# Two copies moved inside ScalarE's odd slots of a graph and attention kernel

## The reference, cut to what matters

```
x = x + gnn(layernorm(x), edges) + mix(layernorm(x))     # 100000 edges, two graph layers
x = x + ffn(layernorm(x))                                # sliced attention
# mix, for each node (it has one position):
h = logmap0(proj(x)); qkv = relu(batchnorm(h @ w_qkv))   # 256 -> 768
s = (t * w_dw) @ w_pw                                    # 768 -> 768, in blocks
o = (v*k).q / v                                          # 512
ft = logmap0(o) @ w_res + b_res                          # 512 -> 256
```

## Time and profile before

| what | value |
|---|---|
| median of 3 runs | 3138.98 us |
| the profiled execution | 3125.24 us, of which the span is 3123.4 us |
| PE busy | 2205.8 us (71%) |
| ACT busy | 1586.5 us (51%) |
| DVE busy | 1539.7 us (49%) |
| POOL busy | 1536.8 us (49%) |
| granted TensorE clock, mean | 0.846 |

### The profile page before, as it was taken

The page is one execution under the profiler, slowest core; times in us unless marked ns, Lnnn a source line. Parts: engine busy times, 40 slices in busy tenths (PEclk is TensorE's granted clock), DMA queues, the critical chain, the costliest instruction groups (busy, mean ns, idle before and its releaser), DMA issues.

```text
span 3123.4 us, 35503 instructions
## 1 busy us (share of the span) xinstructions
PE 2205.8 (71%) x8926; PEld 1604.7 (51%) x8926; DVE 1539.7 (49%) x3687; ACT 1586.5 (51%) x3866; POOL 1536.8 (49%) x1617
## 2 busy tenths in 40 slices
PE   2785668887887877877434567667776666668799
PEld 1563446665665655655323444445544444445558
DVE  8899736665666565655462123323332333334432
ACT  6411357775776756666442444444544445455520
POOL 2000466664665555556635665546655555556300
PEclk9897689997999988988766878888887878889889
DMA  7300233332333333333433333333333333333242
GB/s 187 107 25 17 77 95 100 103 103 79 108 108 96 101 92 94 97 91 97 130 109 90 101 108 91 100 91 101 110 98 90 92 96 93 101 94 112 81 105 75
DMA packets 145156, 300.23 MB, mean 96 GB/s; under 512 B 31588, under 2 KB 89618, under 8 KB 143087
## 3 DMA queue, kind: packets, MB, share of 16 engines
q0 software_dynamic: 75264, 205.62, 22.7%
q10 hardware_dynamic: 52000, 51.21, 5.4%
q1 hardware_dynamic: 17698, 41.13, 4.8%
HBM read 259.44 MB, written 38.40 MB: 95 GB/s over the span
## 4 chain that ended last, share of the span: by engine, by line
PE 29%; DVE 21%; another core or an unknown queue 20%; ACT 16%; issue 11%; ACTq 2%; DVEq 1%; DMA 1%; SPq 0%
PE ps L1443 12%; ACT arena_b L944 5%; ACT whole L946 3%; PE ps L1677 3%; DVE arena_a L1760 3%; PE ps L1576 3%; DVE arena_a L1761 2%; PE ps L1462 2%; DVE whole L2072 2%; PE ps L1581 2%; DVE whole L2126 1%; ACT arena_b L935 1%; PE ps L1560 1%; PE ps L1479 1%
## 5 line engine op out<-in xcount | busy, mean ns | idle before, releaser
L808 POOL DMA_INDIRECT whole<-table,arena_a x1568 | 1517.7, 968 | 1167.5 <-issue 439.1
L1443 PE MATMUL ps<-whole 128*125 x3968 | 1059.5, 419 | 288.4 <-issue 190.1
L1443 PEld LDWEIGHTS ps<-whole 128*125 128x125 f32 x3968 | 811.0, 209 | 490.1 <-issue 355.0
L2072 DVE TENSOR_TENSOR whole<-ps,whole 125x257 f32 (+1 forms) x496 | 210.2, 424 | 1236.2 <-remote 664.5
L944 ACT ACTIVATE arena_b<-iota_row,arena_a 128x125 f32<-128x125 f32 (+1 forms) x1496 | 459.0, 387 | 101.8 <-issue 60.3
L946 ACT ACTIVATE whole<-arena_b,ones 128x1000 f32<-128x1000 f32 (+1 forms) x248 | 279.8, 1128 | 8.8 <-ACT arena_b L944 0.7
L1462 PE MATMUL ps<-arena_b,whole 128*125 128x384 f32 x400 | 183.4, 587 | 0.0
L935 ACT ACTIVATE arena_b<-iota_row,arena_a 128x125 bf16<-128x125 f32 x488 | 153.6, 388 | 37.8 <-issue 32.2
L2126 DVE RECIPROCAL whole<-whole 125x512 f32<-125x512 f32 x50 | 167.7, 3353 | 2.8 <-DVE whole L2125 1.1
L1581 PE MATMUL ps<-arena_b,whole 125*128 125x257 f32 x400 | 106.7, 415 | 30.2 <-DVE whole L2275 29.5
L1576 PE MATMUL ps<-arena_b 128*125 128x512 f32 x200 | 127.7, 771 | 0.0
(11 more groups left out here) (436 smaller groups left out, 3145.8 us busy)
## 6 DMA issues: line engine op xcount, KB each, us to landing
whole<-table,arena_a POOLq DMA_INDIRECT x1568
arena_a<-table ACTq DMA_DIRECT2D x100, 125.0 KB
whole<-xn_rows ACTq DMA_DIRECT2D x50, 125.0 KB
mix_rows<-whole ACTq DMA_DIRECT2D x50, 125.0 KB
table<-whole ACTq DMA_DIRECT2D x50, 125.0 KB
arena_b<-in_x_dram ACTq DMA_DIRECT2D x50, 125.0 KB
arena_b<-mix_rows ACTq DMA_DIRECT2D x50, 125.0 KB
x_rows<-whole ACTq DMA_DIRECT2D x50, 125.0 KB
```

The costliest lines, as they stand in the source:

```text
L808: pool.indirect_dma_start(gat[:, GRP * slot + k, 0:D], None, table[l], bass.IndirectOffsetOnAxis(ap=s_dst[:, n:n + 1], axis=0)).then_inc(s ...
L1443: mm = pe.matmul(ps[0:PT, banks[at % len(banks)], 0:width], onehot[:, ROUND * (r % 2) + QS * k + n, :], gat[:, bass.ds(slots[QS * k + n], ...
L2072: dve.tensor_tensor(to, ps[0:PT, banks[at % len(banks)], 0:width].unsqueeze(1), to, ALU.add).then_inc(s("agg_added"), 1)
```

## The change

Only the source order of ScalarE's `mix_slot` in layer 0 changes. Two copies move, both in odd slots afterwards:

- the copy of the residual products (step 11) stood behind the relu and the copy of `oT`; it now stands ahead of the relu
- the copy of the turned rows with its load (was at `at_slot(i, 2)`, first in the even slot, behind the one-hots of the odd one) is now at `at_slot(i, 1)`, behind the copy of `oT` in the odd slot, ahead of that slot's square of the relu and of its one-hots

The other steps keep their order. No instruction, wait or semaphore is added or removed. The diff, cut where lines only shift:

```diff
 def mix_slot(i, l=l):
-    t = at_slot(i, 2)
-    if t is not None:
-        act.wait_ge(s("hin_turned"), g(t) + 1)
-        if g(t) >= 2:
-            act.wait_ge(s("qkv_made"), g(t) - 1)
-        act.activation(hT_ring[...], ps[:, 6, 0:2 * PT]..., ACT.Copy).then_inc(s("hT_ready"), 1)
-        if t + 2 < NM:
-            load_rows(t + 2)
     t = at_slot(i, 8)
...
     t = at_slot(i, 9)        # square root
...
+    t = at_slot(i, 11)
+    if t is not None:
+        act.wait_ge(s("ft_made"), g(t) + 1)
+        if t >= 2:
+            act.wait_ge(s(f"mix_stored{t % 2}"), 16 * parity_count(t - 2))
+        act.activation(ft[:, t % 2, :], ps[0:PT, 6, D:2 * D], ACT.Copy).then_inc(s("ft_out"), 1)
     t = at_slot(i, 3)        # relu
...
     t = at_slot(i, 9)        # copy of oT
...
-    t = at_slot(i, 11)
-    ...
+    t = at_slot(i, 1)
+    if t is not None:
+        act.wait_ge(s("hin_turned"), g(t) + 1)
+        if g(t) >= 2:
+            act.wait_ge(s("qkv_made"), g(t) - 1)
+        act.activation(hT_ring[...], ps[:, 6, 0:2 * PT]..., ACT.Copy).then_inc(s("hT_ready"), 1)
+        if t + 2 < NM:
+            load_rows(t + 2)
     t = at_slot(i, 3)        # square of the relu's output
```

More of the change, by code:

```diff
@@ L959, in mix_slot @@
                     c = lambda t, k, n=1: sm[:, t % 6, k:k + n]
-                    t = at_slot(i, 2)
-                    if t is not None:
-                        act.wait_ge(s("hin_turned"), g(t) + 1)
-                        if g(t) >= 2:
-                            act.wait_ge(s("qkv_made"), g(t) - 1)
-                        act.activation(hT_ring[:, 2 * (t % 2):2 * (t % 2) + 2, :], ps[:, 6, 0:2 * PT].rearrange("p (k c) -> p k c", k=2), ACT.Copy).then_inc(s("hT_ready"), 1)
-                        if t + 2 < NM:
-                            load_rows(t + 2)
                     t = at_slot(i, 8)
@@ L1013, in mix_slot @@
                         act.activation(oT_ring[:, 4 * (t % 2):4 * (t % 2) + 4, :], ps[:, 2, 0:4 * PT].rearrange("p (k c) -> p k c", k=4), ACT.Copy).then_inc(s("oT_ready"), 1)
-                    t = at_slot(i, 11)
+                    t = at_slot(i, 1)
                     if t is not None:
[L1016 to L1019, removed]
+                        act.wait_ge(s("hin_turned"), g(t) + 1)
+                        if g(t) >= 2:
+                            act.wait_ge(s("qkv_made"), g(t) - 1)
+                        act.activation(hT_ring[:, 2 * (t % 2):2 * (t % 2) + 2, :], ps[:, 6, 0:2 * PT].rearrange("p (k c) -> p k c", k=2), ACT.Copy).then_inc(s("hT_ready"), 1)
+                        if t + 2 < NM:
+                            load_rows(t + 2)
                     t = at_slot(i, 3)
```

## The result

The changed kernel takes 3168.53 us (median of 20 runs, 3148.99 to 3193.91) where the kernel before takes 3135.59 us (20 runs, 3106.41 to 3164.28). The ratio is 1.0134, 95% interval 1.0111 to 1.0157, which is 42 us (35 to 49). The ratios of this document are worked out from the fast runs alone (those within 1.5% of the quickest of their kernel), so that they can differ from the quotient of the medians beside them, which here are 33 us apart. The forecast was 46 us slower, at 3185 us.

A forecast was written before the change was run, and what follows sets the result against it. TensorE was taken to bound undisturbed pairs of slots, ScalarE close behind. 38.5 + 14 - 7 = 45.5, say 46 us, on the profiled 3125.24 gave 3171, and 13.7 us for the median 3185 us; range 3137 to 3224.

The forecast's parts named there:

- The first term: ScalarE's turned-rows copy waits ahead of square and one-hots, delaying line 1460: 1.75 us in 22 pairs, 38.5 us slower.
- rival A: TensorE's qkv products: each of 33 new waits also brings the lower clock, 1.6 us each, 3238 us; chance 0.12.
- The second term: Relu and oT copy queue behind ScalarE's wait for ft_made: 1.3 us in 11 pairs, 14 us slower.
- the give-back of 7 us: TensorE's line 1490 gets the residual copy up to 1.46 us earlier, which counts in 5 of 13 places.
- The signs: Profile after: turned-rows copy waits 50 to 100 us, residual copy over 33.1, line 1490 little; hardly any pair under 17 us.
- B: Mixing stage set by late semaphores and VectorE, so gain and loss cancel: within 6 us of 3139; chance 0.10.
- C: Early residual copy shortens all 13 waits of line 1490, 19 us, and the turned rows' wait vanishes: 3120 us; chance 0.12.

The follow-up runs named there:

- the three depths of the copy: Against the kernel before, quick chip, only the turned rows' copy moved: ahead of the square 1.0230, behind it 1.0014, in the middle of the one-hots 0.9982.
- the second trace: The kernel before, unchanged, profiled again on the chip of a later call for comparison of traces: 3127.99 us, one run.

## Why the prediction was right, and where it wasn't

*What bounds the stage.* The reading that TensorE is the limit in the rounds of the earlier trace rows and that the one-hots lie in the time before `hin_turned` is shown by the three depths of the copy: the idle time falls by what is put ahead of the wait.

*The first term, the copy of the turned rows: 38.5 us, bounds 14 and 57.* Alone it cost 40 us (22 to 59) on a chip like the forecast's. The round of 17.3 us is 17.1 on a bare chip. Its make-up is different, and that the size came so near is in part luck. The forecast had 38.5 us of idle time ahead of line 1460 and nothing for the clock. In the profiled executions, with both halves moved, that idle time grew by 22.6 us and the qkv bursts by 12.9 us (the milder half of rival A, which had 53 us on top), 35.5 us together, of which 30.8 arrive in the length of the 45 rounds. The count of rounds without idle time did go from 22 to 2, but 20 x 1.65 = 33 us would have to be new, and the total grew by less, since the idle times of 3 us and more shrank from 86 to 77 us together. On the quick chip, where every round pays, the same term is 59 us, over a pace that the gathers set.

*The second term, the residual copy ahead of the relu: 14 us of loss and 7 us back.* This step failed. "Where ScalarE is the limit that is paid in full" was wrong: alone, the move gains 19 us on a slow chip (0.9938), and costs nothing on the quick one (0.9995), where few rounds could have shown it. The waits say where the cost isn't. The copy waits longer, 125.0 us in 21 places for late semaphores, and 18.9 us for line 1479. But the late ones are, by their totals, the waits that others had: in the kernel before the relu waited 42.0 us for such semaphores, the copy itself 33.1 and the freeing copy of line 978 54.5, together 129.6 us (135.1 in the second trace), and now it is 125.0 + 8.0 = 133.0. The prediction priced the copy's own wait and left out these two beside it, which are larger. TensorE's idle time ahead of line 1460 fell from 100.5 us (99.4 in the second trace of the kernel before) to 24.3 + 22.6 + 30.4 = 77.3. They also say that the gain isn't where the give-back of 7 us was put: line 1490 still waits 31.5 us for the copy, against 26.9 and, in the second trace of the kernel before, 35.0. Which chain gains the 19 us is not settled; the traces are of different chips, the two of the kernel before differ by 10 us over their 45 rounds, and no run isolates it.

The total came out near, 46 against 42 us, because the first term was right in size and the second was small; that is luck as far as the second goes. Put together from the two halves alone it would have been 40 - 19 = 21 us. The whole change measured 42, 19 (4 to 35) and 37 us (20 to 54) in three comparisons, the last on the chip of the halves: the intervals are too wide to say whether the halves add up.

*The signs.* The copy of the turned rows waits 79.5 us (50 to 100 foretold), no round is under 17 us, the relu no longer waits by itself, and the residual copy waits 119.8 + 22.2 = 142.0 us, over 33.1. The wait of line 1490 for the residual copy did not become small: 32.9 us against 26.9.

*Rivals.* A (each new wait brings the lower clock) happened in part, 9 more slow bursts and not 33. B (the change vanishes in the disturbances) is out, though the same edit cost 40 us with them and 59 without. C (faster) is out for the change. Its first half alone was faster, but not by C's mechanism, since the wait of line 1490 didn't shrink.

*A version better than both.* The residual copy alone ahead of the relu: 0.9938 (0.9895 to 0.9981) on a slow chip, no different (0.9984 to 1.0006) on the quick one. The gain was measured once, as one of several variants, and wants a second measurement.

## What to carry to other kernels

On an engine that works in order, ask of each wait what stands behind it that doesn't need it. The longest independent piece belongs ahead of the wait, in the time in which the other engine prepares the answer; here moving an 0.38 us copy past 4.6 us of such work made each undisturbed round a strict relay between two engines, 17.1 us instead of 15.5. When a change has two halves, run each alone: one of them may be worth keeping.

## What the hardware showed that I hadn't expected

- The same kernel takes 2552 us on one chip and 3117 to 3137 us on others. In the slow traces TensorE's semaphores land up to 17 us after its rows end (in the kernel before, `r_turned` after line 1512's end at 995.0 came at 1009.8), several in a burst; in the quick chip's traces of the two halves they come within 0.02 us. What holds them back isn't shown.
- The size of a change depends on it: the same edit cost 2.3% on the quick chip and 1.3% on a slow one.
- How much idle time goes before a slow burst isn't the same everywhere. On the quick chip 26 idle times of 1.4 to 1.9 us ahead of the qkv products brought none, and 20 of 1.9 to 2.1 us brought 8. In the changed kernel on a slow chip, where longer idle times lie between, idle times of 1.7 us brought some (5.06 us at 800.31 behind 1.69 us), and all 15 of 3 us and more did.
